# Output projection of a graph layer: second half computed tile of rows by tile of rows, with norm, transposes and router logits between

## What is computed

```
x = x + gnn(xn) + mix(xn)            # xn = layernorm(x); gnn ends with out @ wo.T + bo
n2 = layernorm(x)
route_prob = softmax(n2 @ switch_w + switch_b)     # 8 experts, the best one is taken
y = gelu(n2 @ w1[e] + b1[e]) @ w2[e] + b2[e]       # e of the row
x = x + y * max(route_prob)
```

## Time and profile before

| what | us |
|---|---|
| median of 3 runs | 670.26 |
| lowest, highest | 666.72, 671.33 |
| the profiled execution's own time | 665.32 |
| its span in the trace | 663.6 |

### The profile page before, as it was taken

One profiled execution on the slowest core, in us unless ns is written; L12 is line 12 of the kernel. 1 busy time (PEld: TensorE's weight loads), 2 busy tenths in 40 slices (PEclk: granted clock), 3 DMA queues, 4 the chain that ended last, 5 costly groups with the idle time before them and its releaser, 6 DMA issues.

```text
span 663.6 us, 9424 instructions
## 1 busy us (share of the span) xinstructions
PE 581.2 (88%) x3143; PEld 530.8 (80%) x3143; DVE 457.2 (69%) x751; ACT 317.2 (48%) x467; POOL 218.7 (33%) x184
## 2 busy tenths in 40 slices
PE   3899889999999999999998889999799569888860
PEld 2888788888999999998887889999688557676650
DVE  6799997525444554644797878677747947999962
ACT  3455444310333333432745645665435614999950
POOL 5665442555553990600089450000012100000001
PEclk9899999999999999999999999999999759999985
DMA  8476765400346334563222432221254303899925
GB/s 296 137 210 202 185 179 191 133 26 1 103 127 225 121 127 158 161 205 96 63 96 67 137 112 95 63 93 65 96 169 154 111 17 127 313 413 411 411 86 206
DMA packets 32961, 102.68 MB, mean 155 GB/s; under 512 B 5376, under 2 KB 9536, under 8 KB 32928
## 3 DMA queue, kind: packets, MB, share of 16 engines
q1 hardware_dynamic: 27792, 90.02, 40.1%
q0 software_dynamic: 4992, 11.72, 5.7%
q10 hardware_dynamic: 144, 0.52, 0.3%
HBM read 96.65 MB, written 5.60 MB: 154 GB/s over the span
## 4 chain that ended last, share of the span: by engine, by line
PE 57%; DVE 17%; DMA 10%; issue 6%; POOL 4%; ACT 3%; SPq 1%; POOLq 0%; DVEq 0%; ACTq 0%
PE ps L1421 31%; PE ps L1435 8%; DVE wsp L894 5%; DMA rowbuf<-in_dst_rows 5%; DVE big L894 3%; PE ps L1554 3%; DMA raw_x<-in_w_experts 3%; PE ps L1544 2%; PE ps L1649 2%; PE ps L1529 2%; PE ps L1491 2%; PE ps L1472 2%; POOL work L476 2%; PE ps L1564 1%; POOL row_buf L474 1%
## 5 line engine op out<-in xcount | busy, mean ns | idle before, releaser
L1421 PE MATMUL ps<-big,wsp 128*128 128x384 f32 x1680 | 306.4, 340 | 15.9 <-DVE wsp L894 10.9
L1421 PEld LDWEIGHTS ps<-big,wsp 128*128 128x128 f32 x1680 | 294.4, 190 | 24.2 <-DVE wsp L894 9.1
L894 DVE TENSOR_TENSOR wsp<-raw,wsp 128x1024 fp32r<-128x1024 f32 x121 | 164.9, 1377 | 32.2 <-ACT wsp L595 29.8
L595 ACT ACTIVATE wsp<-raw 128x1024 fp32r<-128x1024 f32 x89 | 93.5, 1053 | 41.1 <-PE ps L1435 19.5
L1435 PE MATMUL ps<-wsp,big 128*128 128x512 f32 x288 | 66.7, 391 | 4.0 <-DVE snm L1100 3.5
L494 POOL DMA_INDIRECT edge_table<-ef,eidx x48 | 51.2, 1066 | 50.9 <-DMA edge_table<-ef,eidx 32.4
L1435 PEld LDWEIGHTS ps<-wsp,big 128*128 128x128 f32 x288 | 53.7, 188 | 15.6 <-DVE snm L1100 3.8
L602 ACT ACTIVATE big<-ps,bias 128x384 f32 x24 | 14.0, 583 | 82.5 <-PE ps L1421 82.5
L905 DVE SCALAR_TENSOR_TENSOR big<-ps,bias,big 128x384 f32 x24 | 14.8, 618 | 51.0 <-ACT big L602 50.9
L564 POOL DMA_DIRECT2D slot_y<-maskb x8 | 4.5, 563 | 117.6 <-DVE maskb L1338 117.6
L894 DVE TENSOR_TENSOR big<-raw_x,big 128x1024 fp32r<-128x1024 f32 x32 | 37.8, 1216 | 4.8 <-ACT big L772 4.7
(11 more groups left out here) (230 smaller groups left out, 844.1 us busy)
## 6 DMA issues: line engine op xcount, KB each, us to landing
raw<-in_w_stream SPq DMA_DIRECT2D x89, 512.0 KB
raw_x<-in_w_experts SPq DMA_DIRECT2D x32, 512.0 KB, 6.7
raw<-in_w_experts SPq DMA_DIRECT2D x32, 512.0 KB
rowbuf<-in_src_rows SPq DMA_DIRECT2D x16, 192.0 KB, 4.1
rowbuf<-in_dst_rows SPq DMA_DIRECT2D x16, 192.0 KB, 5.0
rowbuf<-in_rowb POOLq DMA_DIRECT2D x6, 512.0 KB, 6.1
slot_y<-maskb POOLq DMA_DIRECT2D x8, 256.0 KB, 5.5
tok<-in_x SPq DMA_DIRECT2D x3, 512.0 KB, 4.0
```

What stands on the lines that cost most here:

```text
L595: nc.scalar.activation(wsp[:, 0, slot, :], raw[:, slot, :], ACT.Copy).then_inc(w_hi, 1)
L894: return nc.vector.tensor_tensor(dst, value, hi.bitcast(F32), ALU.subtract)
L1421: ins = nc.tensor.matmul(ps[:, bank, 0:N], wsp[:, a, slot, k * P:(k + 1) * P], moving[:, b, k, :], start=(k == 0 and n == 0), stop=(k == K ...
```

## The change

The four quarters of half 1 are loaded into `raw_x` (slots 4 to 7), and the expert stream takes over from slot 0. Half 0 still takes all tiles quarter by quarter; half 1 goes tile by tile (`project(1, t, j)`, 6 matmuls for each quarter and tile). Three quarters of tile 0 run ahead of half 0's last quarter. Tile 0 is transposed before tile 2 is projected; tile 1's transposes and tile 0's logits stand in the middle of tile 2. ScalarE's and VectorE's orders follow: the high and low parts of x2 and single expert splits stand between the steps of the tiles. Six instead of four expert quarters get their low part ahead of the logits, and two fewer get it in the gather of the rows. In the diff, what is only moved or is context is cut.

```diff
--- before.py
+++ after.py
@@ -72,7 +72,7 @@
-WO_ORDER = ((0, 0), (0, 1), (0, 2), (1, 0), (0, 3), (1, 1), (1, 2), (1, 3))
+WO_ORDER = ((0, 0), (0, 1), (0, 2), (0, 3), (1, 0), (1, 1), (1, 2), (1, 3))
@@ -109,9 +109,7 @@
         return q % RING
     if q < Q_WO:
         return 1 + (q - Q_PAIR) % 3
-    if q < Q_MOE:
-        return (q - Q_WO) % RING
-    return (q - Q_MOE + RING) % XRING
+    return (q - Q_WO) % XRING
...
@@ -375,8 +374,11 @@
-            for q in range(Q_WO, Q_MOE):
+            for q in range(Q_WO, Q_WO + RING):
                 load(q * P, slot_of(q), q - RING + 1)
+            sp.wait_ge(w_started, Q_WO - 1)
+            for q in range(Q_WO + RING, Q_MOE):
+                sp.dma_start(raw_slot(slot_of(q)), w_stream[q * P:(q + 1) * P, :]).then_inc(raw_in[slot_of(q)], 16)
             def load_expert(row, k, split):
@@ -384,15 +386,14 @@
                 sp.dma_start(raw_slot(k), w_experts[bass.ds(row, P), :]).then_inc(raw_in[k], 16)
-            sp.wait_ge(w_started, Q_WO + 1)
             for j in range(RING):
-                load_expert(j * P, RING + j, Q_WO)
+                load_expert(j * P, j, Q_MOE + j - XRING + 1)
             with sp.Fori(0, EXPERTS - 1) as i:
                 for k in range(XRING):
                     first = QE + k if k < RING else k
                     row = sp.snap(i * (QE * P) + first * P)
-                    load_expert(row, k, i * XRING + (Q_MOE + RING + k - XRING + 1))
+                    load_expert(row, (RING + k) % XRING, i * XRING + (Q_MOE + RING + k - XRING + 1))
             q = Q_MOE + QE * EXPERTS - RING
             for j in range(RING):
...
@@ -755,35 +756,31 @@
                 acc_part(feat[0][head_rows(s), 0, PAIRS - 1, :], head_rows(s), 0.0)
-            for q in range(Q_WO + 4, Q_MOE):
-                prep(slot_of(q))
+            def prep_x(started=None):
+                slot = slot_of(q_no.n)
+                act.wait_ge(raw_in[slot], used[slot].add(16))
+                act.wait_ge(w_started, q_no.value - (XRING - 2) if started is None else started)
+                nc.scalar.activation(split_of(slot, 0), raw_slot(slot), ACT.Copy).then_inc(w_hi, 1)
+                q_no.add()
+            for _ in range(RING):
+                prep_x(Q_WO + 1)
             act.wait_ge(b12_in, 32)
             act.wait_ge(b12_zero, 1)
             for first in (0, 32):
                 rows = slice(first, first + EXPERTS)
                 nc.scalar.activation(b12r[rows, :], work[rows, 0:F + D], ACT.Copy).then_inc(b12_hi, 1)
-            def prep_x(wait=True):
-                slot = (q_no.n - Q_MOE + RING) % XRING
-                act.wait_ge(raw_in[slot], used[slot].add(16))
-                if wait:
-                    act.wait_ge(w_started, q_no.value - (XRING - 2))
-                nc.scalar.activation(split_of(slot, 0), raw_slot(slot), ACT.Copy).then_inc(w_hi, 1)
-                q_no.add()
             for _ in range(RING):
                 prep_x()
-            act.wait_ge(wo_ready, 2 * NT)
-            for _ in range(RING):
-                prep_x(False)
             nc.scalar.activation(tri_r, cst[:, C_TRI:C_TRI + 2 * P], ACT.Copy).then_inc(tri_set, 1)
             def x2t_copy(t):
                 act.wait_ge(x2t_ready, t + 1)
-                nc.scalar.activation(x2t[t], set_banks_row(t), ACT.Copy).then_inc(x2t_copied, 1)
+                nc.scalar.activation(x2t[t], whole(x2t_banks(t)), ACT.Copy).then_inc(x2t_copied, 1)
...
+            act.wait_ge(b12_lo, 1)
             x2t_copy(0)
             split_x2(0)
+            prep_x()
             x2t_copy(1)
+            split_x2(1)
+            prep_x()
             x2t_copy(2)
-            split_x2(1)
             split_x2(2)
+            prep_x()
+            act.wait_ge(wo_ready, 2 * NT)
+            prep_x(Q_MOE)
             act.wait_ge(lmax_done, 1)
...
@@ -1207,22 +1220,24 @@
+            for _ in range(2):
+                prep_x()
             for t in range(NT):
                 dve.wait_ge(mix_done, t + 1)
                 projected(0, t)
-            for _ in range(2):
-                prep_x()
             projected(1, 0)
+            prep_x()
+            normalised(0)
+            prep_x()
             projected(1, 1)
-            normalised(0)
+            split_x2(0)
+            normalised(1)
+            prep_x()
             projected(1, 2)
-            normalised(1)
             dve.wait_ge(b12_lo, 1)
             normalised(2)
-            for _ in range(2):
-                prep_x()
+            split_x2(1)
+            prep_x()
@@ -1234,18 +1249,6 @@
...
-            split_x2(0)
-            split_x2(1)
             dve.wait_ge(logits_ready, 1)
...
@@ -1339,7 +1342,7 @@
             for k in range(KT):
                 got_low(k)
-                if k % 2:
+                if k in (1, 3):
                     prep_x()
             routes()
             prep_x()
...
@@ -1592,37 +1595,76 @@
             pair()
-            def project(h, j):
-                token_major(slot_of(Q_WO + WO_ORDER.index((h, j))), j, feat[0], 5 - 3 * h, wo_ready)
-            pe.wait_ge(s_max, HEADS)
-            project(0, 0)
-            transpose_probs(0)
-            project(0, 1)
-            pe.wait_ge(acc_free, acc.value)
-            attend(0)
-            transpose_probs(1, 2)
-            project(0, 2)
-            attend(1)
-            project(1, 0)
-            pe.wait_ge(acc_free, acc.value)
-            for h, j in WO_ORDER[4:]:
-                project(h, j)
-            pe.wait_ge(wo_sum, 2 * NT)
-            for t in range(NT):
+            def project(h, t, j):
+                for kk in range(2):
+                    k = 2 * j + kk
+                    for n, (a, b) in enumerate(PASSES):
+                        ins = nc.tensor.matmul(ps[:, 5 - 3 * h + t, :], feat[0][:, b, k, t * P:(t + 1) * P],
+                                               split_of(slot_of(Q_WO + h * RING + j), a)[:, kk * HALF:(kk + 1) * HALF],
+                                               start=(k == 0 and n == 0), stop=(k == KT - 1 and n == 2))
+                        if kk == 0 and n == 0:
+                            first = ins
+                if j == 3:
+                    ins.then_inc(wo_ready, 1)
+                return first
+            def project_all(j):
+                open_quarter()
+                for t in range(NT):
+                    first = project(0, t, j)
+                    if t == 0:
+                        first.then_inc(w_started, 1)
+            def transpose_x2(t):
                 pe.wait_ge(x2_done, t + 1)
                 for k in range(KT):
-                    ins = nc.tensor.transpose(set_banks(t)[:, k, :], x2[t][:, k * P:(k + 1) * P], ident)
+                    ins = nc.tensor.transpose(whole(x2t_banks(t))[:, k * P:(k + 1) * P],
+                                              x2[t][:, k * P:(k + 1) * P], ident)
                 ins.then_inc(x2t_ready, 1)
-            for t in range(NT):
+            def logits(t):
                 pe.wait_ge(x2t_copied, t + 1)
                 for k in range(KT):
                     ins = nc.tensor.matmul(ps[:, 1, t * EXPERTS:(t + 1) * EXPERTS], x2t[t][:, k * P:(k + 1) * P],
                                            swt[:, k, :], start=(k == 0), stop=(k == KT - 1))
-            ins.then_inc(logits_ready, 1)
+                return ins
+            pe.wait_ge(s_max, HEADS)
+            project_all(0)
+            transpose_probs(0)
+            project_all(1)
+            pe.wait_ge(acc_free, acc.value)
+            attend(0)
+            transpose_probs(1, 2)
+            project_all(2)
+            attend(1)
+            for j in range(3):
+                pe.wait_ge(w_lo, Q_WO + RING + j + 1)
+                project(1, 0, j)
+            pe.wait_ge(acc_free, acc.value)
+            project_all(3)
+            pe.wait_ge(w_lo, Q_MOE)
+            project(1, 0, 3).then_inc(w_started, 1)
+            for j in range(RING):
+                project(1, 1, j)
+            pe.wait_ge(wo_sum, NT)
+            transpose_x2(0)
+            for j in range(RING):
+                first = project(1, 2, j)
+                if j:
+                    first.then_inc(w_started, 1)
+                if j == 1:
+                    transpose_x2(1)
+                    logits(0)
+            q_no.add(RING)
+            logits(1)
+            transpose_x2(2)
+            logits(2).then_inc(logits_ready, 1)
             pe.wait_ge(tri_set, 1)
             pe.wait_ge(hot_done, 1)
             for t in range(NT):
@@ -1706,12 +1748,12 @@
             pe.wait_ge(fold_set, 1)
             pe.wait_ge(got_hi, KT)
             pe.wait_ge(got_lo, KT)
-            up(0, 0, RING)
+            up(0, 0, 0)
             for e in range(EXPERTS - 1):
-                up(e + 1, e + 1, 0, (lambda: hidden(0)) if e == 0 else None)
-                down(e, e, RING)
+                up(e + 1, e + 1, RING, (lambda: hidden(0)) if e == 0 else None)
+                down(e, e, 0)
```

(35 more changed lines are left out.)

## The result

The changed kernel takes 671.42 us (median of 15 runs, 670.18 to 674.39); the kernel before, run on the same chip, 665.95 us (15 runs). The ratio is 1.0075, 95% interval 1.0057 to 1.0093: a small loss, under the 1% named in the prediction, with an interval that excludes no change. The profiled execution took 670.21 us with a span of 668.5 us.

A forecast was written before the change was run, and what follows sets the result against it. TensorE waiting on VectorE's chain, to 522.4, then TensorE's own transposes and logits, to 534.7, bound the kernel. Logits 5.5 us later (540.2 against 534.7) on the 670.3 median gave 675.8 us; range 668.0 to 681.5, forecast case 673.8 to 678.3.

The forecast's parts named there:

- First gap: Before half 1's matmuls, TensorE waits 3.0 us for the first quarter's low part and starts at 497.0.
- Constants stalled by GpSimd: VectorE's constants, started at 500.6, again meet GpSimd's bias instruction L556 (501.7 to 505.3) and end at 507.3.
- Root held by a split: Before tile 0's norm, a 1.2 us VectorE split holds GpSimd's L447 until 516.5; without the hold, 0.7 us less.
- Second gap: After 66 matmuls end at 512.1, TensorE idles 6.0 us for normalised tile 0, until 518.1; clock likely falls.
- Last matmul at 530.1: End of the projection: after tile 1's transposes, tile 0's logits and 12 matmuls (2.75 us), TensorE is at 530.1.
- Logits read at 540.2: The last tile's logits end at 540.2, against 534.7 in the kernel before: 5.5 us later.
- The tail of one tile: Behind the projection, the last tile goes alone through sum, root, norm, transposes, copy and logits: 10 us.
- What it spends: 3.0 + 6.0: Up to the logits, the change spends 3.0 + 6.0 + about 1 us of waits, then a 10 us serial tail.
- The clock came back 3.1 us after TensorE restarted; with the same here: After the second gap, the clock is back at 521.2; three matmuls run at some 0.42 us, nine at 0.229.
- The clock is low when the gather starts, now as before: In the gather behind routing, the clock starts low in both kernels, so no difference was counted there.
- All of the 5.5 us reaches the end: Behind the logits, two fewer splits in the gather and the loads gain nothing, so 5.5 us stay in the total.
- not slower: Rival, chance 0.08: VectorE keeps ahead, first norm ready by about 512; the floor is -5.0, 665.3 us.

The follow-up runs named there:

- a3: Changed kernel with tile 0's norm moved ahead of the expert split that stood between its statistics and its norm: 671.44 us, 1.0051 of the kernel before.
- a1: Changed kernel with VectorE's block of constants moved ahead, behind its first attention split of the last pair: 669.29 us, 1.0053 of the kernel before.
- b1: Kernel before with the block of constants moved ahead of VectorE's last four splits, run twice: 660.62 us (0.9917), then 660.22 us (0.9895).
- a2: Changed kernel with half 0's last quarter (18 matmuls) run ahead of half 1's three quarters for tile 0: 671.21 us, 1.0089 of the kernel before.
- a7: a5 with half 0's last quarter also run ahead of half 1, as in a2: 664.25 us, 0.9941 of the kernel before.
- a5: Changed kernel with the constants moved as in a1 and all six expert splits behind tile 0's norm: 669.81 us, 1.0036 of the kernel before.
- a4: Changed kernel with 20, 8 and 4 unread matmuls ahead of tile 0's transposes, ahead of tile 2's and behind them: 668.8 us, 1.003 of before.
- b2: b1 with unread matmuls, 8 ahead of the transposes, 5 and 10 in the routing, run twice: 0.9904, then 0.9864 (658.11 us) of the kernel before.

## Why the prediction was right

I predicted 675.8 on a median of 670.3, that is +0.8%; it is +0.75%. The 671.42 itself lies below the 673.8 to 678.3 that I gave this case, since the median of the first three runs was 4.3 us above that of all fifteen, 665.95. Most steps were right too, with these sizes (predicted, measured):

- First gap 3.0, 2.92. Splits done at 500.5, 500.1. Constants stalled by GpSimd, done at 507.3; 506.8. The instruction that met L557 was the tensor_scalar L1210, not the cast.
- Root held by a split: held, L448 1.01 us. Norm done at 518.0; TensorE had it at 517.53. The Trainium skill, "SBUF — State Buffer", section "SBUF: two separate sides", says that a VectorE instruction with two SBUF inputs and a GpSimd instruction that reads SBUF exclude each other for their whole length. The trace agrees, here, in a3 (1.08 us) and the other way round in a1 and b1, where splits waited for GpSimd.
- Second gap 6.0, 5.56. The clock fell in it, 3.8 us behind the last matmul, where I had taken 4.8 from the trace before. I had misread that: a mean of 0.55 in 519 to 520 puts the fall at 519.1, 4.5 us behind.
- Last matmul at 530.1, 529.0. Tile 2's last logits at the low clock, 3.56, 3.58. Logits read at 540.2, 539.52, that is +4.8 instead of +5.5 (+5.1 when counted from the attention copy, which came 0.3 us earlier).
- The tail of one tile, 10 us: 10.5.

Steps that failed or were mis-sized:

- "What it spends: 3.0 + 6.0" counts the first gap as a cost. a2 shows that it cost nothing in this kernel: VectorE's path, not TensorE's, set the first norm. The sum of moments was not touched, since it took the later of the two paths.
- "The clock came back 3.1 us after TensorE restarted; with the same here". The 3.1 was misread, too: a mean of 0.54 in 525 to 526 puts the return at 525.9, 3.5 us behind the restart. In the changed kernel it took about 5.1 us, so most of the 12 matmuls ran slow: 4.62 us where I had 3.4. Tile 1 came earlier all the same (norm done at 523.5 for 524.3), because tile 0's transposes began 0.6 us earlier and its low part could start at 521.58, so VectorE reached tile 1's norm at 522.72.
- "The clock is low when the gather starts, now as before": it is, but it returned 5.7 us into the gather, and before after 3.6. The gather took 13.90 us instead of 12.89: +1.0 that I costed at nothing.
- "All of the 5.5 us reaches the end". The experts started 5.8 us later and the span is 4.9 us longer. The trace before has low clock in its last expert, the one after has not:

```profile
637.00:640.00 3.00, 2.25 (x7) 1.82 (x8) 2.74 (x4) 1.88 (x2) 0.55 (x1) 0.76 0.39 87
640.00:643.00 3.00, 3.00 (x11) 2.34 (x10) 0.32 (x1) 0.00 (x0) 0.00 (x0) 0.67 0.03 5
```

```profile
642.00:645.00 3.00, 1.70 (x7) 1.43 (x8) 2.75 (x4) 2.39 (x4) 0.55 (x1) 1.00 0.26 57
645.00:648.00 3.00, 2.68 (x12) 1.88 (x10) 0.86 (x1) 0.28 (x1) 0.00 (x0) 1.00 0.16 36
```

The first is the kernel before, the second the changed one, the same work 5 us later. Whether the change did that or the execution is open. The two errors, +1.0 and -0.9, nearly cancel. That is luck: the total is better than its parts.

Of the rivals, "not slower" had the mechanism right: it needed VectorE ready by about 512 and named 529.7 for the logits, 35.5 us behind the attention copy. a7 has its first norm done at 509.1 and reads its logits at 36.44, with the last products slow. It did not happen in this change, since the constants met the same instruction. What I had not weighed is that the same cure gives the old order more: 5.6 us in b1, against 2.95 in a1. The transposes of three finished tiles in one burst cost little once they start in time. Tile by tile hides about 6 us of TensorE's transposes and products (an estimate, two tiles at 1.1 + 1.85 us), but its last tile still needs sum, root, norm, transposes, copy and products in a row behind the last matmul: 10.5 us in the changed kernel.

## What to carry to other kernels

When the busiest engine waits at a stage's end, find what the engine it waits for did in the 10 us before. Here small constants and two prefetch splits stood ahead of the sums, and moving one block in the old order gave 1%, where the rewrite lost 0.75%. Interleaving pays only if the interleaved step's inputs are ready before TensorE comes to it; else the wait blocks the matmuls queued behind. Here it did not beat the old order even then. A gap ahead of a stage may be free in one version and on the path in the next, so try its removal again after each cure.

## What the runs showed of the hardware

- A cast, a tensor_scalar or a split on VectorE that meets GpSimd's bias instruction waits for the whole rest of it: 3.54 us for the cast before, 3.57 for a tensor_scalar of 8 columns in the changed kernel, 4.71 for two splits of 2.35 in a1. Moving one away hands the wait to the next in line, unless that is a sum or its statistics: in a5 GpSimd's instruction ran from 503.16 to 506.69, and beside it the sum, which reads PSUM, and the statistics, which have one input in SBUF, kept their 0.69 us:

```profile
503.16 3.53 POOL L557 TENSOR_TENSOR big<-work,big 8x1536 fp32r<-8x1536 f32 x1 [10.07 <-ACT big L774]
...
504.54 0.69 DVE L1201 TENSOR_TENSOR tok<-tok,ps 128x512 f32<-128x512 f32 x1 [2.53 <-PE ps L1608]
505.26 0.69 DVE L1203 BATCH_NORM_STATS2 stats<-tok 128x6 f32<-128x512 f32 x1
```

- The clock fell while TensorE was busy without a pause (a5, 0.64 and 0.51), among transposes and 128 x 8 products, and the same sequence in a7 kept 1.00. The last pause before it, 1.36 us, had ended 2.3 us earlier. It also fell at the end of a gap of 2.27 us in b1, and in or behind the first gap of 2.92 us in a1, a3 and a4 (the 18 matmuls behind it took 6.00, 7.18 and 5.82 us) but not in the changed kernel and a5 (4.35 and 4.42). And it fell around a gap of 3.47 us ahead of the projection in some executions and not in others. In the changed kernel:

```profile
474.46 5.99 PE L1603 MATMUL ps<-wsp,big 128*128 128x512 f32 x18 [3.47 <-DVE snm L1103]
```

and in a7, behind the same gap:

```profile
476.77 4.39 PE L1608 MATMUL ps<-wsp,big 128*128 128x512 f32 x18 [3.47 <-DVE snm L1103]
```

The kernel b2 alone took 5.79 us there in one of its profiles and 4.39 in the other. So 1.6 us of a difference between two profiles there is no effect of an edit, and one profile does not tell what the clock does in a kernel; only medians do.
- The clock came back 3.5 and 3.6 us after a restart of TensorE in the kernel before (transposes, gather), 5.1 and 5.7 us in the changed one. I found no single number for it.
